# A 16-head attention beside a mixture-of-experts layer: score matmuls put side by side with maximum matmuls of the other half of the rows, and values taken two steps back

## The reference

```python
xn = _layernorm(x, axis=-1)
# attention
q = (xn @ Wq + bq).reshape(B, S, H, Dh)          # B, S, H, Dh = 2, 1024, 16, 8
latent = xn @ Wl + bl                            # 32 wide
k = (latent @ Wk + bk).reshape(B, S, H, Dh)
v = (latent @ Wv + bv).reshape(B, S, H, Dh)
scores = jnp.einsum('bihd,bjhd->bhij', q, k) * SCALE
attn = jax.nn.softmax(scores, axis=-1)
out = jnp.einsum('bhij,bjhd->bihd', attn, v).reshape(B, S, D) @ Wo + bo
# experts
logits = xt @ Wg.T + bg
top_vals, top_idx = jax.lax.top_k(logits, 2)
gate, up = (xt @ Wgu + bgu)[..., ::2], (xt @ Wgu + bgu)[..., 1::2]
gated = (clip(up, -7, 7) + 1) * gate * sigmoid(1.702 * gate)   # gate cut at 7
out_e = gated @ Wd + bd                          # mixed by the softmax of the two logits
```

## Time and profile before

| | |
|---|---|
| median of 3 runs | 520.67 us (517.59 to 520.69) |
| the profiled execution's own time | 515.9 us |
| its span | 514.0 us |
| PE busy | 453.2 us, 88% |
| DVE busy | 374.6 us, 73% |
| ACT busy | 309.4 us, 60% |
| POOL busy | 192.9 us, 38% |

### The profile page before, as it was taken

The page is one execution under the profiler, slowest core; times in us unless marked ns, Lnnn a source line. Parts: engine busy times, 40 slices in busy tenths (PEclk is TensorE's granted clock), DMA queues, the critical chain, the costliest instruction groups (busy, mean ns, idle before and its releaser), DMA issues.

```text
span 514.0 us, 8995 instructions
## 1 busy us (share of the span) xinstructions
PE 453.2 (88%) x2681; PEld 209.3 (41%) x2681; DVE 374.6 (73%) x725; ACT 309.4 (60%) x356; POOL 192.9 (38%) x240
## 2 busy tenths in 40 slices
PE   0998984998989899989898989898989889799885
PEld 0554441333434344444444444444444434353243
DVE  8479992768888888888888878888888776764011
ACT  1541022477777686768686868686868644448840
POOL 6035876004141414141414141414141461824870
PEclk9976557789999999999999999999999988979966
DMA  8465512500544655304502443041004020101200
GB/s 239 126 120 179 101 44 87 162 3 1 129 123 121 189 102 111 104 1 78 109 22 83 86 100 104 3 82 22 21 3 91 16 59 7 39 22 43 57 23 25
DMA packets 39298, 39.01 MB, mean 76 GB/s; under 512 B 4998, under 2 KB 34792, under 8 KB 38376
## 3 DMA queue, kind: packets, MB, share of 16 engines
q1 hardware_dynamic: 35808, 33.74, 26.3%
q0 software_dynamic: 2432, 4.72, 3.9%
q10 hardware_dynamic: 1032, 0.23, 0.3%
HBM read 23.73 MB, written 13.89 MB: 73 GB/s over the span
## 4 chain that ended last, share of the span: by engine, by line
PE 59%; POOL 11%; DVE 11%; ACT 8%; issue 6%; another core or an unknown queue 2%; DMA 1%; ACTq 0%; SPq 0%; DVEq 0%; POOLq 0%
PE banks L987 17%; PE banks L970 16%; PE banks L1035 11%; DVE half_max L810 7%; ACT probs L674 5%; PE banks L1056 3%; PE banks L1054 3%; POOL th L545 2%; POOL up L546 2%; POOL up L528 2%; PE banks L1019 1%; PE banks L1017 1%; POOL th L544 1%; POOL up L541 1%
## 5 line engine op out<-in xcount | busy, mean ns | idle before, releaser
L810 DVE TENSOR_REDUCE half_max<-banks 128x1 f32<-128x512 f32 x512 | 322.0, 685 | 52.9 <-PE banks L970 39.9
L674 ACT ACTIVATE probs<-banks 128x1024 f32<-128x1024 f32 x256 | 254.9, 1026 | 162.5 <-PE banks L1035 113.1
L970 PE MATMUL banks<-k_rows,q_rows 62*128 62x512 f32 x512 | 182.9, 484 | 14.6 <-DVE half_max L810 10.4
L1035 PE MATMUL banks<-q_rows,k_rows 64*128 64x512 f32 x512 | 141.7, 460 | 7.0 <-ACT probs L674 5.5
L987 PE MATMUL banks<-probs,v_pad 128*32 128x512 f32 x1024 | 142.4, 630 | 0.0
L970 PEld LDWEIGHTS banks<-k_rows,q_rows 62*128 62x128 f32 x512 | 87.9, 199 | 103.5 <-DVE half_max L810 72.0
L1035 PEld LDWEIGHTS banks<-q_rows,k_rows 64*128 64x128 f32 x512 | 63.1, 192 | 77.6 <-ACT probs L674 66.9
L528 POOL TENSOR_TENSOR gate<-gate,w_blk 128x512 f32<-128x512 f32 x12 | 12.6, 1048 | 108.3 <-ACT gate L658 108.3
L528 POOL TENSOR_TENSOR up<-up,w_blk 128x512 f32<-128x512 f32 x12 | 12.6, 1049 | 97.8 <-ACT up L660 97.8
L510 POOL DMA_INDIRECT x_table<-xn,place_u x32 | 31.1, 972 | 20.9 <-DVE place_u L792 11.5
L987 PEld LDWEIGHTS banks<-probs,v_pad 128*32 128x32 f32 x1024 | 20.7, 110 | 44.3 <-issue 35.3
(11 more groups left out here) (117 smaller groups left out, 345.2 us busy)
## 6 DMA issues: line engine op xcount, KB each, us to landing
w_blk<-in_wexp SPq DMA_DIRECT2D x48, 193.0 KB, 3.1
q_rows<-q_parts SPq DMA_DIRECT2D x28, 128.0 KB
k_rows<-k_parts SPq DMA_DIRECT2D x56, 64.0 KB
x_table<-zeros SPq DMA_DIRECT2D x1, 3072.0 KB, 12.5
x_rows<-x_table SPq DMA_DIRECT2D x12, 256.0 KB, 3.7
moe_table<-x_rows SPq DMA_DIRECT2D x12, 256.0 KB, 6.8
q_parts<-q SPq DMA_DIRECT2D x8, 256.0 KB
k_parts<-k SPq DMA_DIRECT2D x8, 256.0 KB
```

What stands on the lines that cost most here:

```text
L674: nc.scalar.activation(probs[:, (2 * s + part) % 4, :, :], banks[:, bank:bank + 2, :], ACT.Exp, scale=SCALE).then_inc(slot_free, 1)
L810: nc.vector.tensor_reduce(half_max[:, unit, row, half:half + 1], banks[:, ring_bank(job), :], AX_X, ALU.max).then_inc(ring_free, 1)
L970: pe.matmul(bank, q_rows[slot][rows, pair, q0:q0 + P], k_rows[slot][rows, pair, 512 * keys:512 * keys + 512], start=True, stop=True).then_ ...
L1035: mm = pe.matmul(banks[:, bank + u, :], k_rows[(unit // 2) % 2][rows, pair, P * kb:P * kb + P], q_rows[(unit // 2) % 2][rows, pair, 512 * ...
```

## The change

On PE the order within a pair of steps becomes

The core of the diff (left out: the same counts of jobs and slots in SP, POOL and in `OUT_JOB`, 5 to 8 and 3 to 4):

```diff
 def max_place(n):
 
-    return n // 16, n // 4 % 4, n // 2 % 2, n % 2
+    return n // 16, n // 4 % 4, n // 2 % 2, 1 - n % 2
+
+
+def prob_slot(s):
+
+    return s % 3 if s < STEPS + 2 * HEAD - 2 else (s + 1) % 3
+
+
+def values_done(s):
+
+    return s - 2 if s < STEPS + 2 * HEAD - 2 else s - 1
...
-        attnT = sb("attnT", [P, 512])
...
+        attnT = xT_blk
...
-        probs = sb("probs", [P, 4, 2, 512])
+        probs = sb("probs", [P, 6, 2, 512])
...
             def exps(base, slot, t, s, part):
                 act.wait_ge(slot_full, base + slot + 1)
-                if s >= 2:
-                    act.wait_ge(s_pv, STEPS * t + s - 1)
+                if s >= 3:
+                    act.wait_ge(s_pv, STEPS * t + values_done(s))
                 bank = 2 * (slot % 2)
-                nc.scalar.activation(probs[:, (2 * s + part) % 4, :, :], banks[:, bank:bank + 2, :], ACT.Exp,
+                nc.scalar.activation(probs[:, 2 * prob_slot(s) + part, :, :], banks[:, bank:bank + 2, :], ACT.Exp,
                                      scale=SCALE).then_inc(slot_free, 1)
 
             def pair(base, slot, t, p, last):
                 exps(base, slot, t, 2 * p, 0)
                 exps(base, slot + 1, t, 2 * p, 1)
+                exps(base, slot + 2, t, 2 * p + 1, 0)
                 if p % 4 == 0 and p > 0:
                     keep_pv(t, p // 4 - 1)
                 if tanh_group(p, last) is not None:
                     tanh_of(t, tanh_group(p, last))
-                exps(base, slot + 2, t, 2 * p + 1, 0)
+                exps(base, slot + 3, t, 2 * p + 1, 1)
                 if has_item(p, last):
-                    item_in(base, slot + 3, t, *item_of(p, last))
-                exps(base, slot + 3 + has_item(p, last), t, 2 * p + 1, 1)
+                    item_in(base, slot + 4, t, *item_of(p, last))
...
-                for n, (ahead, m) in enumerate(maxima[:5]):
+                for n, (ahead, m) in enumerate(maxima):
                     max_job(base, job + n, ahead, m)
-                job += len(maxima[:5])
+                job += len(maxima)
...
-                for n, (ahead, m) in enumerate(maxima[5:]):
-                    max_job(base, job + n, ahead, m)
...
-            def scores(base, slot, s, pair, t):
+            def scores(base, slot, s, pair, t, jbase, job, maxima):
+
                 unit, kb = divmod(s, KB)
                 half = unit % 2
                 if kb == 0 and pair == 0:
@@ -1034,7 +1044,10 @@
                     rows = slice(64 * u, 64 * u + ROWS)
                     mm = pe.matmul(banks[:, bank + u, :], k_rows[(unit // 2) % 2][rows, pair, P * kb:P * kb + P],
                                    q_rows[(unit // 2) % 2][rows, pair, 512 * half:512 * half + 512], start=True, stop=True)
-                mm.then_inc(slot_full, 1)
+                    if u == 1:
+                        mm.then_inc(slot_full, 1)
+                    if maxima:
+                        max_job(jbase, job + 2 * pair + u, s + LEAD, 2 * pair + u)
...
-                scores(sbase, slot, a, 0, t)
+                scores(sbase, slot, a, 0, t, jbase, job, maxima)
+                if p > 0:
+                    values(sbase, slot - 2, t, a - 2)
+                scores(sbase, slot + 1, a, 1, t, jbase, job, maxima)
+                scores(sbase, slot + 2, b, 0, t, jbase, job + 4, maxima)
+                if p > 0:
+                    values(sbase, slot, t, b - 2)
+                scores(sbase, slot + 3, b, 1, t, jbase, job + 4, maxima)
+                if has_item(p, last):
+                    item(sbase, slot + 4, t, *item_of(p, last))
                 if maxima:
-                    max_job(jbase, job, a + LEAD, 0)
-                scores(sbase, slot + 1, a, 1, t)
-                if maxima:
-                    max_job(jbase, job + 1, a + LEAD, 1)
-                    max_job(jbase, job + 2, a + LEAD, 2)
-                if p > 0:
-                    values(sbase, slot, t, a - 1)
-                if maxima:
-                    max_job(jbase, job + 3, a + LEAD, 3)
-                scores(sbase, slot + 2, b, 0, t)
-                if maxima:
-                    max_job(jbase, job + 4, b + LEAD, 0)
-                    job += 5
-                if has_item(p, last):
-                    item(sbase, slot + 3, t, *item_of(p, last))
+                    job += 8
...
-                    job += 1
-                if maxima:
-                    max_job(jbase, job, b + LEAD, 1)
-                    max_job(jbase, job + 1, b + LEAD, 2)
-                scores(sbase, slot + 3 + has_item(p, last), b, 1, t)
-                if maxima:
-                    max_job(jbase, job + 2, b + LEAD, 3)
-                values(sbase, slot + 2, t, a)
...
-            values(sbase, slots_before(PAIRS, HEAD, True), TURNS - 1, STEPS - 1)
+            slot = slots_before(PAIRS, HEAD, True)
+            values(sbase, slot - 2, TURNS - 1, STEPS - 2)
+            values(sbase, slot, TURNS - 1, STEPS - 1)
```

More of the change, by code:

```diff
@@ L312, in moe_attention_kernel @@
         last_jobs = jobs_before(PAIRS, HEAD, True)
-        OUT_JOB = {2 * b + half: jobs_before(p + 1, HEAD, True) + (5 if has_max(p + 1, True) else 0) + turned_jobs(p + 1, True) - 1
+        OUT_JOB = {2 * b + half: jobs_before(p + 1, HEAD, True) + 8 * has_max(p + 1, True) + turned_jobs(p + 1, True) - 1
                    for p, (b, half) in PROJECT.items()}
@@ L420, in turn @@
                         unit = (2 * p + LEAD - 2) // KB
-                        store_max(sp, unit, job_base(t) + jobs_before(p, HEAD, last) + (5 if has_max(p, last) else 0))
+                        store_max(sp, unit, job_base(t) + jobs_before(p, HEAD, last) + 8 * has_max(p, last))
                         load_max(sp, unit, 4 * t + unit + 1)
@@ L437, in turn @@
                         i = item_of(p, last)[1]
-                        store_rows(SLOTS * t + i, slot + 3)
+                        store_rows(SLOTS * t + i, slot + 4)
                         if i == SLOTS - 1:
@@ L583, in pair @@
                     fill_v(2 * t + 3, 1)
-                slot = slot_base(t) + slots_before(p, HEAD, last) + 3
+                slot = slot_base(t) + slots_before(p, HEAD, last) + 4
                 if has_item(p, last):
@@ L694, in _ @@
                     unit = (2 * p + LEAD - 2) // KB
-                    store_max(act, unit, AHEAD_JOBS + jobs_before(p, 0, False) + 5)
+                    store_max(act, unit, AHEAD_JOBS + jobs_before(p, 0, False) + 8)
                     load_max(act, unit, unit + 1)
@@ L987, in values @@
                     mm = pe.matmul(banks[32 * j:32 * j + 32, 4, :], v_pad[:, (unit // 2) % 2, kb, j, :],
-                                   probs[:, (2 * s + j // 2) % 4, j % 2, :], start=(kb == 0), stop=(kb == KB - 1))
+                                   probs[:, 2 * prob_slot(s) + j // 2, j % 2, :], start=(kb == 0), stop=(kb == KB - 1))
                 mm.then_inc(s_pv, 1)
```

## The result

The median of the changed kernel is 533.3 us (four runs: 532.9, 532.9, 533.7 and 541.4), of the kernel before, run beside it, 520.7 us (517.6 to 522.5). A few runs of most kernels here are slower than the others and show a lower granted TensorE clock (the 541.4 is one, at .905 against .919 to .923); the medians in this document are over all runs, and the ratios leave the slow ones out. The ratio is 1.025, 95% interval 1.018 to 1.031: slower, clear of the noise, but whether by more than 2% stays open. The forecast was 535 us and a ratio of 1.028. The profiled execution has a span of 531.1 us against 514.0, 17.1 more.

A forecast was written before the change was run, and what follows sets the result against it. PE was taken as the bound (59% of the chain). Full ring, fourth exponential and other pair terms gave +4.80 a turn, +14.4 over three: 515.9 to 530.3 profiled, ratio 1.028, so 535 us median, range 517 to 545.

The forecast's parts named there:

- PE's list one step shorter: PE's own list per pair: 8 couples or singles instead of 9, one step of .23 less, 5.78 to 5.56 us.
- Values two steps back: Value matmuls on PE: they never waited for probabilities before, so taking them two steps back gains nothing.
- The full ring: M5 waits .48 for M2's bank, values restart .42 behind it; the pair loses .57, against .23 won.
- The fourth exponential: At a pair's end on ACT: the next pair's first scores wait for it, so an ordinary pair takes 6.30 us.
- Kept values and tanh ahead of it: ACT at p = 8, 12, 16: they delay the fourth exponential, so these pairs take 6.52 us.
- Turned values: Pairs p = 5, 9, 13, 17: PE's list decides, with .43 for the transposes, 6.56 us.
- POOL's chain: Up item to turned maximum 8.53, to down item 7.88: 7.22 us at p = 6, 10, 14, 7.66 at p = 18.
- The sum of a turn: All sixteen pairs of a turn: 106.62 us against 101.82, +4.80, times three turns +14.4.
- The last turn: Turn without items: ring could cost up to 4.0 or win 1.6 us; taken as 0.
- PE's list alone: Rival: each pair .23 shorter and no wait grows, 11.0 us gained, median 510; chance .11.
- the ring that doesn't stop PE: Rival: fourth exponential limits pairs, other waits stay, -.42 a turn, median 519; chance .13.

The follow-up runs named there:

- a5: Changed kernel without the swap of halves: each maximum job uses the half of the score matmul before it; 524.04 us, kernel before 488.45 on the same chip.
- b4: Kernel before with only the swap: maximum jobs use the other half of the rows, no instruction moves; ratio 1.001 (.995 to 1.006).
- a1: Changed kernel, but DVE reduces only 256 of 512 columns of each pair's third maximum job (M2); 505.56 us, kernel before 488.45 on the same chip.
- a2: Changed kernel with maximum job M5 moved behind values(b-2) on PE; 510.04 us, kernel before 491.15 on the same chip.
- a7: a8 plus M5 moved behind values(b-2), as in a2; ratio 1.004 (1.001 to 1.008) to the kernel before.
- a8: Changed kernel, PE's order untouched, with POOL's earlier split, kept values and tanh behind the fourth exponential, and earlier row loads; ratio 1.023 to the kernel before.
- a3: Changed kernel with ACT's fourth exponential ahead of the kept values and the tanh; 513.02 us, kernel before 488.45 on the same chip.
- a6: Changed kernel with POOL splitting the finished maxima in the middle of the up work; 514.90 us, kernel before 491.15 on the same chip.
- b1: Kernel before with POOL splitting the finished maxima in the middle of the up work; ratio .995 (.992 to .998).
- a4: Changed kernel with SP starting the loads of the next q and k rows one slot earlier; 512.46 us, kernel before 488.45 on the same chip.
- b2: b1 plus ACT's third exponential ahead of the kept values and the tanh; ratio .992 (.989 to .995) to the kernel before.
- b3: b2 with POOL's old order kept at p = 17 and 18; ratio .990 (.984 to .996) to the kernel before.

## Why the prediction was right, step by step

**PE's list one step shorter: right in size, wrong in its reason.** I counted couples in the order of the list. By a5 and b4 the halves run as two lists. The count comes out the same here, because the change puts two matmuls of each half ahead of the first values, four ahead of the second and two behind them (8), where before the fuller half had 4, 2 and 3 (9). That both ways of counting agree is luck. The swap of the halves, which looks like the point of the change, does nothing (b4). With it falls what I took from the Trainium skill ("TensorE: Matmul & The Clock Gate", Part 3), that matmuls never pass each other: a5's rows contradict it for matmuls of different halves. What holds in the rows shown is the weaker statement that the argument needed: nothing passes a matmul that is stopped at its own wait. The values stay behind M5 (266.31 and 266.74), and at 276.26, where the score matmul waits for ACT, the job behind it uses the other half, has had a free bank since 275.87 at the latest (274.58 + 1.29) and still starts at 276.34.

**Values two steps back: nothing to give.** Right in the pairs read: they start behind PE's own work both before and after (257.17, and 266.74 after). The one place where they show is p = 18, where the exponential waits for them (312.78).

**The full ring: right.** M5 waits .47 (forecast .48), the values follow by .43 (.42). Confirmed by a1, a2 and a7 against a8; on the net size, .34 forecast and .33 measured a pair, the last one is the cleanest. It costs more than the step that the order wins.

**The fourth exponential: right in place, .07 too dear.** It starts .42 behind the last score matmul, not .51, so p = 11 takes 269.58 - 263.35 = 6.23 instead of 6.30.

**Kept values and tanh ahead of it: right, .16 too cheap.** p = 12 takes 276.26 - 269.58 = 6.68 against 6.52. Of this .08 is that the first job of a pair starts .08 behind its score matmul when PE comes out of a wait for ACT (269.58 and 269.66), which I had not read. a3 measures the step itself: .35 a period, .45 expected.

**Turned values: .09 too cheap.** p = 13 takes 282.91 - 276.26 = 6.65 against 6.56, and .08 of it is the same late first job (276.34). The .43 for the transposes holds (281.38 to 282.91 is 1.53).

**POOL's chain: right.** At p = 14 the turned maximum comes 8.56 behind the up item (281.38 to 289.94), forecast 8.53. At p = 18 of turn 2 the down item comes 7.88 behind the up item (416.40 to 424.28), as forecast. But I read the 7.88 of the earlier trace rows as POOL's, while the bracket names the exponential: before the change POOL is done there at 405.74 and ACT at 405.79, with PE at 405.86, so both bind. a6 and b1 show that it swallows what PE gains in that period. My term took POOL's work as given; it was the nearest thing to be had, 1.03 a period (b1).

**The sum of a turn: too small.** Forecast +4.80, measured +5.66 in turn 2. The mid-turn periods were .17 too small (26.60 forecast, 26.77), the one across the turn's border .44 (26.38 and 26.82). The latter is the first job of the turn, which waits for the copy of the turned maximum (318.45 above): p = 3 takes 324.66 - 318.01 = 6.65 instead of 6.30, and p = 5 has the .09 of the turned values. The period of p = 18 was right in turn 2 (27.04 and 27.11) and failed in turns 0 and 1 by .7 to .8: that is **the missed term**. I wrote that SP gets the same transfers, and did not follow what each waits for. SP waits for the last slot of the pair before, and that slot is now the item at the pair's end. Before, the first load goes out at 286.09, 1.11 ahead of the start of its pair (287.20); after, it goes out with it (296.39 and 296.38), and PE waits 1.11 for the keys at p = 18. a4 shows that an earlier start removes that wait. The later start is not all: from the first load to the first score matmul of p = 18 pass 13.90 before (286.09 to 299.99), without a wait, and 14.49 after (to 310.88), so the loads themselves took at least .5 longer in turn 1, and why stays open.

**The last turn: 0 forecast.** From the last of the twelve periods to the end the kernel takes 1.3 less (105.8 and 107.2). PE's granted clock differs there between the two executions (.57 from 443 to 458 us after; the lowest of five such stretches before is .74), so this says little about the order.

So 3.6 us too little in the loop and 1.3 too much behind it (and .4 too little ahead of it) partly cancel, which is luck, and the profiled ratio came out at 1.033 against a forecast of 1.028. The medians lie lower (1.025): the profiled run before, 515.9, was faster than each of its timed ones.

**The rivals.** PE's list alone (faster) fails at M5's wait, and the ring that doesn't stop PE (no change) too. a7 comes near that second one, with the ring wait gone at the price of one step, so that its list has nine steps again. With the other waits mended as well it is 2.9 us a turn better than before the change, but no better than b2 and b3 (98.88 against 98.97 and 98.65 in turn 2), which have the old order on PE. So the gain comes from the other mends, and the order gives next to nothing even without its ring wait. Eight steps without a ring wait, which would want a fourth bank, was not built.

## What to carry to other kernels

When work is regrouped so that matmuls stand closer together, count the buffers that a group takes before counting the steps that it saves: four jobs on three banks wait for a whole reduction, and all that is behind them waits too. Look at the borders of a loop too, where a bank that is dealt out by number can meet its own last user. Look up for every DMA that is moved or not moved which event starts it, because the event may have moved. And ask first which engine's chain swallows the gain: two moves off PE's list (POOL's split, ACT's order) gave .8 to 1.0% where the new PE order lost 2.5%.

## What the runs showed of the hardware

- Matmuls on rows 0 to 63 and on rows 64 to 127 are served as two lists: for a list of half 0, 0, 1, 1 the starts are 344.37, 344.70, 344.38, 344.72 in a5; and a swap of halves over a whole kernel changes its time by .1%, within the noise of .6% (b4).
- Behind a stop on a semaphore PE restarts slower than it runs: the values start .43 behind a job that has waited and .32 behind one that has not, and behind a wait for ACT the other half starts .08 late (276.26 and 276.34).
- A DVE reduction of 512 columns takes .685, of 256 columns .425 (a1). From these two, .165 of it does not depend on the columns, an estimate that takes the rest as proportional to them.
- The same kernel (before) takes 488 to 491 us on three chips and 514 and 521 in the runs on others. Its own trace exists from one chip only, but b2 and b3 differ in little and ran on a chip of each kind: turn 2 takes 98.97 and 98.65 us, while from the first turned maximum to the second pass 24.3 and 32.4 us (granted clock .71 and .63), and from the last period to the end 92.6 and 102.4. A difference of a per cent is read from runs on one chip, or from the periods.
